# Layer b of a two-layer hybrid kernel: which engine's row holds the copy of the attention sums out of PSUM

## The reference

```python
x = x + attn_a(_layernorm(x), Wq, bq, Wk, bk, Wv, bv, Wo, bo)   # layer a: 32 heads of 8, softmax over all keys
x = x + ffn(_layernorm(x), w_gate, w_up, w_down)                # silu(gate)*up, 2 of 4 kept, down
x = x + attn_b(_layernorm(x), wq, wk, wv, wo)                   # layer b
x = x + ffn(_layernorm(x), w_gate, w_up, w_down)

# attn_b: 32 query heads, 8 key and value heads (4 query heads share one)
scores = jnp.einsum('bhqd,bhkd->bhqk', q, k) / jnp.float32(np.sqrt(HD))
amask = jnp.where((j >= i - W) & (j < i), jnp.float32(-10000000000.0), jnp.float32(0.0))   # W = 128
attn = jax.nn.softmax(scores + amask[None, None, :, :], axis=-1)
out = jnp.einsum('bhqk,bhkd->bqhd', attn, v).reshape(Bb, Ll, Dm)
return out @ wo
```

## Time and profile before

| | |
|---|---|
| median of 3 runs | 1772.51 us (1772.0 to 1775.72) |
| the profiled execution, device time | 1771.24 us |
| its span in the trace | 1769.5 us |
| layer b's attention in steady work | about 994 to 1546 us of the span |
| PE / DVE / ACT / POOL busy over the span | 95% / 84% / 72% / 14% |

### The profile page before, as it was taken

The page is one execution under the profiler, slowest core; times in us unless marked ns, Lnnn a source line. Parts: engine busy times, 40 slices in busy tenths (PEclk is TensorE's granted clock), DMA queues, the critical chain, the costliest instruction groups (busy, mean ns, idle before and its releaser), DMA issues.

```text
span 1769.5 us, 39224 instructions
## 1 busy us (share of the span) xinstructions
PE 1688.9 (95%) x13872; PEld 660.9 (37%) x13872; DVE 1489.3 (84%) x2158; ACT 1282.4 (72%) x2424; POOL 253.1 (14%) x609
## 2 busy tenths in 40 slices
PE   7799999999999999999987999999999999999999
PEld 4222222222222223777653222222222222247777
DVE  6899999999899992676777899999999999926655
ACT  3279999999899998333222899999989999973221
POOL 1210000000000000000001222233332223320000
PEclk9889999999999999999996999999999999999999
DMA  8824533333443312200305222222322222111000
GB/s 229 291 53 75 83 71 59 65 59 68 83 81 59 64 33 61 60 1 0 110 14 139 52 49 48 54 48 54 71 57 55 48 54 48 44 54 51 13 12 24
DMA packets 72124, 114.67 MB, mean 65 GB/s; under 512 B 12464, under 2 KB 27824, under 8 KB 71984
## 3 DMA queue, kind: packets, MB, share of 16 engines
q1 hardware_dynamic: 71984, 112.63, 28.7%
HBM read 71.96 MB, written 40.63 MB: 64 GB/s over the span
## 4 chain that ended last, share of the span: by engine, by line
PE 50%; DVE 35%; issue 9%; DMA 2%; ACT 1%; DVEq 1%; SPq 1%; POOL 0%; POOLq 0%; ACTq 0%
DVE mneg L1102 21%; PE psum L714 13%; PE psum L654 12%; DVE xn L1108 11%; PE psum L636 9%; PE psum L734 6%; PE psum L609 5%; PE psum L694 2%; PE psum L577 1%; DVE mneg L1108 1%; DMA k_stacks<-area 1%; DVEq L1098 1%; DMA max_rows<-mT 1%; DMA q_stacks<-area 1%; PE psum L622 1%
## 5 line engine op out<-in xcount | busy, mean ns | idle before, releaser
L888 ACT ACTIVATE area<-psum 128x512 f32<-128x512 f32 x2048 | 1108.5, 599 | 99.8 <-PE psum L636 75.9
L654 PE MATMUL psum<-area 128*32 128x256 f32 x8192 | 643.1, 392 | 0.7 <-POOL area L1340 0.4
L636 PE MATMUL psum<-area 51*128 51x512 bf16 x2048 | 638.8, 386 | 3.6 <-DMA area<-max_rows 2.8
L1108 DVE CUSTOM_DVE_ANT_0 xn<-psum,band 128x1024 f32<-128x1024 f32 x512 | 592.8, 1220 | 34.3 <-PE psum L609 33.8
L1102 DVE TENSOR_REDUCE mneg<-psum 128x1 f32<-128x1024 f32 x512 | 586.1, 1216 | 23.6 <-PE psum L609 23.6
L609 PE MATMUL psum<-area 48*128 48x512 bf16 x1024 | 297.7, 392 | 23.6 <-DVE mneg L1102 23.3
L654 PEld LDWEIGHTS psum<-area 128*32 128x32 f32 x8192 | 169.0, 108 | 385.6 <-issue 245.1
L609 PE MATMUL psum<-k_max_b,area 48*128 48x512 bf16 x1024 | 288.8, 389 | 23.7 <-DVE mneg L1108 22.9
L636 PEld LDWEIGHTS psum<-area 51*128 51x128 bf16 x2048 | 137.2, 94 | 456.4 <-ACT area L888 414.6
L931 ACT ACTIVATE area<-psum 128x512 f32<-128x512 f32 x64 | 38.2, 597 | 158.8 <-PE psum L714 158.8
L714 PE MATMUL psum<-xnT,wg 128*128 128x512 f32 x256 | 122.3, 600 | 1.5 <-ACT xnT L846 1.5
(11 more groups left out here) (70 smaller groups left out, 823.1 us busy)
## 6 DMA issues: line engine op xcount, KB each, us to landing
ctx_rows<-area SPq DMA_DIRECT2D x64, 256.0 KB, 2.1
area<-q_stacks SPq DMA_DIRECT2D x32, 384.0 KB, 7.7
area<-k_stacks SPq DMA_DIRECT2D x64, 192.0 KB, 6.8
area<-q_stacks_b SPq DMA_DIRECT2D x32, 384.0 KB, 5.9
area<-q_stacks SPq DMA_DIRECT2D x32, 192.0 KB, 4.2
area<-q_stacks_b SPq DMA_DIRECT2D x32, 192.0 KB, 3.3
area<-ctx_rows SPq DMA_DIRECT2D x16, 256.0 KB, 4.6
area<-inv_rows SPq DMA_DIRECT2D x16, 256.0 KB, 5.6
```

The costliest lines, as they stand in the source:

```text
L636: pe.matmul(psum[:, S_BANKS[slot % len(S_BANKS)], :], k_st[lo:lo + ROWS + PARTS, buf, 0 if a else head // 2, kt * P:(kt + 1) * P], q_st[lo ...
L654: mm = pe.matmul(psum[head * VW:(head + 1) * VW, PV_BANK, cols], vaug[:, buf, kt, head, :], probs[:, u % PRING, head, cols], start=(kt == ...
L888: act.activation(probs[:, u % PRING, head, :], psum[:, S_BANKS[slot_of(u, head, ahead) % len(S_BANKS)], :], ACT.Exp, scale=SCALE).then_inc ...
L1108: dve.tensor_tensor_reduce(band_out[:, c % 2, :], slot, band[:, at:at + SEQ], 1.0, -3.0e38, ALU.add, ALU.max, mneg[:, qh, col:col + 1]).th ...
```

## The change

In layer b 31 of the 32 copies go from ACT's row to DVE's; only the very last (group 15, qh = 1) stays with ACT. The copy of a group's half qh = 1 stands ahead of maximum c = 4 of the next turn, that of qh = 0 ahead of c = 20. Its waits are the same (`pv_done`, `ctx_stored`), and so is what it signals. Group 14's second half comes behind the last maximum, ahead of `divide_ctx`; group 15's first half behind the two `divide_ctx`. Layer a stays as it was.

```diff
+COPY_AT = 2 * LAG
+        def copied_by_dve(a, g, qh):
+            return a == 1 and not (isinstance(g, int) and g == GROUPS - 1 and qh == 1)
...
             def copy_ctx(a, g, qh):                       # ACT
+                if copied_by_dve(a, g, qh):
+                    return
...
-            def group(a, g):                              # DVE
+            def copy_ctx(a, g, qh):
+                n = HALF * (GROUPS * a + g) + qh
+                dve.wait_ge(pv_done, UNITS * (GROUPS * a + g) + (qh + 1) * BT)
+                dve.wait_ge(ctx_stored, 16 * (n - 1))
+                dve.tensor_copy(ctx_sb[:, qh, :], psum[:, PV_BANK, :]).then_inc(ctx_copied, 1)
+
+            def group(a, g, first=False):
                 for c in range(CHUNKS):
+                    if a == 1 and not first and c == COPY_AT:
+                        copy_ctx(a, g - 1, 1)
+                    if a == 1 and c == CPH + COPY_AT:
+                        copy_ctx(a, g, 0)
                     maxima(a, g + 1, c)
...
-                group(a, 0)
+                group(a, 0, first=True)
...
+                if a == 1:
+                    copy_ctx(a, GROUPS - 2, 1)
                 divide_ctx(a, 0)
                 divide_ctx(a, 1)
+                if a == 1:
+                    copy_ctx(a, GROUPS - 1, 0)
```

## The result

The changed kernel takes 1786.52 us (median of 13 runs, 1777.72 to 1789.54) against 1772.62 us for the kernel before beside it. The ratio of the runs is 1.0069, 95% interval 1.0054 to 1.0084: 12.2 us slower, with 9.6 to 14.9 as the bounds (the two medians are 13.9 us apart). The profiled execution took 1784.08 us, its span is 1782.4.

A forecast was written before the change was run, and what follows sets the result against it. Bound: layer b's 19.13 us period, 4.25 on PE's path plus 14.88 on DVE. 29 x 0.33 = +9.6, less 0.25 for the last group, +9.3 on 1771.24, plus 1.27 for the median: 1781.8 us, range 1776 to 1790.

The forecast's parts named there:

- rival C: Layer b's steady periods: each grows by the copy's whole 0.61 us, +17.4 us in all, 1789.9 us; chance 0.08.
- The copy's price: DVE between two maxima: the copy takes 0.61 us of DVE's row, its result there 0.69 us after its start.
- The delay of the block: Layer b's block of 16 products waits for DVE's copy, 0.33 us later per period; 29 periods, +9.6 us.
- the release: Start of PE's 4.25 us path in each period: maximum 3 is done at 1203.99 and PE goes on.
- DVE's gaps: DVE's two waits behind the block, for maxima 6 and 7: 0.815 us per period, shrinking to 0.54.
- PE's path: From maximum 3's release through the block to DVE's refilled bank pairs: 4.25 us of the 19.13 us period, growing by 0.33.
- ACT: Behind the block: 29 steady copies taken off ACT gain nothing; its idle time grows from 0.60 to about 1.1 us.
- The last group: End of layer b: block after group 14's products starts near 1549.32 in place of 1549.57, -0.25 us; group 15's copy nothing.
- A: Between the block and maximum 7: ACT's earlier exps shorten PE's path to 4.04 us, -6.3 us, 1766.2 us; chance 0.06.
- B: DVE's copy runs at twice the rate, 0.42 us; the block waits 0.02 us, +0.3 us, 1772.8 us; chance 0.06.

The follow-up runs named there:

- PE's new order: The kernel before, with each max_scores behind the block of 16 products one place earlier in PE's row, both layers: 1758.69 us, ratio 0.9925.
- The second kernel: The changed kernel with DVE's copy one maximum later, ahead of c = 5 and c = 21: 1889.38 us in one run.

## Why the prediction was right

Forecast: 1781.8 us, +9.3, range 1776 to 1790. Measured: 1786.5, and +12.2 by the ratio. The range took in rival C's 1789.9 as well, so the time alone doesn't tell the forecast from C; the traces do. The mechanism is the one forecast, and shown by taking it apart: DVE's row time without the wait costs nothing, ACT's time given back changes nothing, and a copy 0.27 us shorter costs 0.27 us less a step.

- *The copy's price.* 0.69 us and 0.60 of DVE's row; forecast 0.69 and 0.61, from the earlier trace rows. Right.
- *The delay of the block.* This is the term that was sized too small. I took 0.33 us as the middle between a signal answered in 0.06 us, as after a maximum in the earlier trace rows, and in 0.15, as after ACT's copy in the earlier trace rows. Measured 0.38 against the release, 0.37 a step. The answer to DVE's copy took 0.15 us for both lengths of it (and 0.14 where it came one maximum later). The row that is like it in kind (a copy releasing the products) was the better guide than the one that shares the engine. Worth 29 x 0.04 = 1.2 us. It also puts the block 0.84 us after the copy's start, where I had named 0.75.
- *DVE's gaps.* Forecast 0.54 us left of 0.815, found (1033.76 - 1032.35 - 1.145) + (1035.24 - 1033.76 - 1.145) = 0.60, with 1032.35 as the start of maximum 5. The period is PE's path plus 14.88 us on DVE, as said. (The longer step at the reciprocal, which I put at some 1.7 us more, is 1.61 more.)
- *ACT.* Idle for 1.30 us behind the block; forecast about 1.1. No gain, as said.
- *The last group.* Forecast -0.25 us, found +0.2: this term has the wrong sign. The first block came 0.11 us nearer than before; the second, at 1582.24, 0.30 us later after it (20.11 in place of 19.81), and so it is, to 0.04, in every run with DVE's copies whose chain shows it. ACT is idle at another point there; which order of its exps makes the 0.30 I haven't shown.
- *What wasn't in the sum.* The granted clock. It was 0.50 of full speed for some 10 us of the profiled execution, worth some 3.4 us, and the step behind the reciprocal was another 0.35 longer. In 13 runs the mean clock is on average 0.9775 against 0.9783 in 58 runs of the kernel before (those of all comparisons). At the same clock the difference is 11.2 us, against 12.2 in all. That would leave about 1 us of the mean to the clock, but one step of 0.001 in the clock goes with about 1.2 us, so this can't be told from chance. With 29 x 0.37, the last group's 0.2 and the 0.35 the path makes 11.3.

Of the rivals, A (ACT's relief) is excluded by the run that gave its time back, B (twice the rate) by the copy, which took 684 to 691 ns all 31 times though it writes a dense row, C (the whole copy shows) by DVE's idle copy that cost nothing. C's price is what the copy costs in the kernel with PE's new order, where DVE's gap stands elsewhere.

## What to carry to other kernels

Here the copy out of PSUM cost what its end did to the next writer of the bank, as long as a gap of its new engine stood behind it; with the gap elsewhere its whole row time showed. So before moving one, find what releases that writer now, and put the copy's end on the new engine against it: here ACT was done 0.2 us before the release and DVE 0.7 us after it. And where an engine has gaps in front of a full queue of its own, look at the order of the engine that feeds it: its reordering gained about as much (13.3 us) as the move of the copy lost (12.2).

## What the runs showed of the hardware

Where PE's waits grew, more was lost than their length. Steps in which PE waits 0.36 and 0.30 us kept the full clock, save at the reciprocal. With one wait of 1.30 us in a step, five of 28 steps had the clock fall to half, at 1.2 to 2.7 us each; with one of 1.45 us (and one of 0.36 ahead of it), 23 of 28, at 2.5 to 4.3 us each. The second kernel was thereby some 70 us slower than its lengthened path explains. The single waits of 1.12 and 1.22 us at the reciprocals were followed by a fall in 6 of 14 cases. The waits are what differs between these kernels; that they alone bring the fall isn't shown, since the same wait in the same code went with a fall in one trace and without one in another.
